# In the first layer, ScalarE makes the normalised input between the two exponentials of head six, and VectorE copies the fourth turn ahead of the low half of the source

## The reference, cut to what matters

```python
x = _gn(x)                                  # group norm, then in the layer:
x = _layernorm(x1d, norm_w, norm_b)         # per token
qkv = (x @ qkv_w.T).reshape(*x.shape[:-1], c, 3 * h)     # c = 32, h = 8 heads
q, k, v = (qkv[..., :h], qkv[..., h:2 * h], qkv[..., 2 * h:])
aff = jnp.einsum('bmich,bmjch->bmijh', q, k)
gate = jax.nn.sigmoid(x @ gate_w.T + gate_b).reshape(*x.shape[:-1], c, h)
bias = x2d @ x2d_w.T * factor
weights = jax.nn.softmax(aff + bias[:, None], axis=-2)
out = jnp.einsum('bmrch,bmirh->bmich', v, weights) * gate
out = out.reshape(*x.shape[:-1], c * h) @ final_w.T + final_b
```

## Time and profile before

| | |
|---|---|
| time, three runs | 3560.49 us median (3558.21 to 3562.08) |
| the profiled execution | 3560.76 us, span 3558.9 us |
| busy share of the span | PE 95%, PEld 84%, DVE 83%, ACT 77%, POOL 61% |
| mean granted TensorE clock | 0.971; 1.00 in both layers' steady stretches |
| DMA, mean over the span | 67 GB/s |

### The profile page before, as it was taken

How to read it: one execution, slowest core, us unless ns; L and a number is a source line. 1 busy time by engine, 2 the same in 40 slices (tenths; PEclk the granted TensorE clock), 3 DMA queues, 4 the chain that set the end, 5 groups by cost and what they waited for, 6 DMA issues and landing times.

```text
span 3558.9 us, 123057 instructions
## 1 busy us (share of the span) xinstructions
PE 3369.3 (95%) x36747; PEld 3001.8 (84%) x36747; DVE 2968.9 (83%) x10850; ACT 2753.6 (77%) x8999; POOL 2165.3 (61%) x4107
## 2 busy tenths in 40 slices
PE   4569999999999999999999999799999999999999
PEld 1148888888888888888888887799999999999998
DVE  4569999999999999999999998688888888888886
ACT  1149999999999999999999998567766667766666
POOL 0048888888888888888888886344444444443443
PEclk7579999999999999999999999899999999999999
DMA  9921111111111111111111111111111111111111
GB/s 356 370 91 54 53 48 49 53 50 48 53 53 44 53 53 46 51 53 53 44 53 53 44 53 34 42 51 53 53 53 53 50 50 53 53 53 53 51 49 49
DMA packets 189033, 238.42 MB, mean 67 GB/s; under 512 B 11825, under 2 KB 176177, under 8 KB 184753
## 3 DMA queue, kind: packets, MB, share of 16 engines
q1 hardware_dynamic: 184368, 204.17, 18.2%
q10 hardware_dynamic: 4608, 33.56, 2.5%
HBM read 170.57 MB, written 67.11 MB: 67 GB/s over the span
## 4 chain that ended last, share of the span: by engine, by line
PE 71%; DVE 9%; issue 8%; ACT 6%; DMA 4%; POOL 1%; DVEq 1%; SPq 0%; ACTq 0%; POOLq 0%
PE work L477 26%; PE work L486 11%; PE turn L538 7%; PE score L629 5%; PE score L508 5%; PE mix L662 4%; PE mix L550 4%; DMA x_chunk<-xT 4%; DVE prob L936 3%; ACT prob L734 3%; PE turn L646 3%; PE score L538 2%; ACT xnT L754 2%; PE turn L647 2%; PE turn L648 2%
## 5 line engine op out<-in xcount | busy, mean ns | idle before, releaser
L364 POOL TENSOR_SCALAR prob<-prob,row_inv 128x256 f32<-128x256 f32 x2048 | 1029.0, 522 | 213.0 <-DVE row_inv L942 211.5
L734 ACT ACTIVATE prob<-prob,row_min 128x256 f32<-128x256 f32 x2048 | 1022.0, 508 | 68.0 <-DVE row_min L936 61.4
L477 PE MATMUL work<-src,w 128*128 128x256 f32 x7680 | 1062.7, 287 | 10.3 <-DVE src L925 6.7
L477 PEld LDWEIGHTS work<-src,w 128*128 128x128 f32 x7680 | 946.9, 189 | 12.1 <-DVE src L925 7.4
L415 POOL TENSOR_SCALAR prob<-prob,row_inv 128x160 f32<-128x160 f32 x1024 | 391.1, 401 | 767.8 <-DVE row_inv L1055 767.8
L936 DVE CUSTOM_DVE_ANT_0 prob<-score,neg_bias 128x256 f32<-128x256 f32 x2048 | 756.9, 417 | 48.9 <-PE score L508 46.6
L799 ACT ACTIVATE prob<-prob,row_min 128x160 f32<-128x160 f32 x1024 | 431.2, 426 | 142.7 <-DVE row_min L1048 142.6
L538 PE MATMUL turn<-ident,prob 128*128 128x128 f32 x3072 | 471.9, 276 | 11.4 <-DVE probT L947 2.6
L486 PE MATMUL work<-w,src 128*128 128x256 f32 x3072 | 427.9, 288 | 9.7 <-ACT xnT L754 7.4
L477 PE MATMUL work<-att,wf 128*128 128x256 f32 x3072 | 432.6, 290 | 4.0 <-DVE att L1006 2.6
L538 PEld LDWEIGHTS turn<-ident,prob 128*128 128x128 f32 x3072 | 342.9, 141 | 85.0 <-POOL prob L364 45.3
(11 more groups left out here) (112 smaller groups left out, 6118.5 us busy)
## 6 DMA issues: line engine op xcount, KB each, us to landing
pair_chunk<-pairT ACTq DMA_DIRECT2D x32, 1024.0 KB, 7.7
x_chunk<-xT SPq DMA_DIRECT2D x32, 1024.0 KB, 8.4
x_tok<-x_nat SPq DMA_DIRECT2D x128, 256.0 KB, 3.3
x_sb<-xT SPq DMA_DIRECT2D x128, 256.0 KB, 3.4
x1T<-y_sb SPq DMA_DIRECT2D x128, 256.0 KB, 2.2
x_sb<-x1T SPq DMA_DIRECT2D x128, 256.0 KB, 2.9
outT<-y_sb SPq DMA_DIRECT2D x128, 256.0 KB, 2.2
prob<-w_d SPq DMA_DIRECT2D x1, 1024.0 KB, 8.2
```

What stands on the lines that cost most here:

```text
L364: pool.tensor_scalar(prob[:, h, ib], prob[:, h, ib], row_inv[:, h, ib:ib + 1], 1.0, ALU.mult, ALU.mult).then_inc(norm_done[0], 1)
L477: ins = pe.matmul(out[:, cb], w[:, of_w, kb, cols + cb * P:cols + (cb + 1) * P], x[:, of_x, kb], start=n == 0, stop=n == len(terms) - 1)
L734: act.activation(prob[:, h, ib], prob[:, h, ib], ACT.Exp, bias=row_min[:, h, ib:ib + 1], scale=-1.0, accum_out=row_sum[:, h, ib:ib + 1]).t ...
```

## The change

Two things are reordered, and nothing is added or removed. On ScalarE `exps(m, 5)` is split: its first half stays, `xnT` follows, and the second half comes after `xnT`, ahead of the key's high half. On VectorE the copy of turn 3 comes ahead of `split_low(0, far, ...)`. (Head six in the title counts from one: it is head 5 of the code.)

```diff
-                def exps(r, h):
-                    for ib in range(TB):
+                def exps(r, h, blocks=range(TB)):
+                    for ib in blocks:
...
-                    exps(m, 5)
+                    exps(m, 5, (0,))
                 if far.exists:
                     wait(act, t2_done, far.times(1, 1))
                     wait(act, src_done[0], far.times(1, 0))
...
                                        ).then_inc(xnT_done, 1)
+                if m.exists:
+                    exps(m, 5, (1,))
                 if nxt.exists:
                     wait(act, k_ps[0], nxt.times(1, 1))
...
+                if m.exists:
+                    turn_copy(3, turn[:])
                 if far.exists:
                     split_low(0, far, xnT[:])
-                if m.exists:
-                    turn_copy(3, turn[:])
                 if nxt.exists:
                     mins(nxt, 0)
```

## The result

The changed kernel takes 3679.8 us (median of 4 runs, 3679.03 to 3682.43) against 3559.35 us for the kernel before on the same chip: a ratio of 1.0338, 95% interval 1.0325 to 1.035. That is +120 us; forecast was +128 us, 3689 us. The profiled execution has a span of 3677.9 us.

The account below looks back on a forecast made before the run. TensorE was taken as nearly the bound, with turn 6 set by the row's first minimum. Collisions on VectorE and GpSimd make a pair of rows 33.26 us against 31.19: +2.07 times 62 pairs, +128 us, 3689 us; range 3575 to 3710.

Parts of the forecast that it names:

- What bounds the kernel: TensorE nearly the bound, busy 61.42 of 62.37 us; VectorE's slack before the row's first minimum leads to turn 6.
- The ScalarE edit: xnT 0.49 us earlier on ScalarE removes the value projection's wait: 0.28 us a row, 35 us at most.
- The displaced exponential: Head 5's second exponential starts 0.90 us after xnT; in rows 1 and 3 inverse at s (turn 6) + 9.90.
- TensorE's clock: From turn 6 (s): turn 2 at s + 9.41 or 9.38, turn 3 1.85 later; source's low half ready s + 12.57 or 12.54.
- GpSimd's clock: L380 starts at s + 12.08 and 12.38, 0.49 and 0.16 us before the source's low half is ready.
- rival 1: One of two effects missing: L925 wins in rows 2 and 4, 3633 us, or head 6's norm first, 3627; chance 0.20.
- The price of a collision: Source's low half waits out L380: next minimum at L380 + 1.76 us; price up to 1.07 us, the upper taken.
- The attention's low half: L1006 starts 1.53 us after the minimum and delays head 6: 2.64 us to turn 6 instead of 2.14.
- The sum: Rows of 16.48 and 16.78 us, a pair 33.26 against 31.19: +2.07, times 62 pairs, +128 us.
- Rival 3: No collision with L380 and none with L1006: a pair 30.77, 3535 us, lower bound 3526; chance 0.14.
- Rival 2: Source's low half not held up, L1006 still delays head 6: a pair 31.77, +36 us, 3597 us; chance 0.09.

Follow-up runs that it names:

- psum: Three timing-only kernels, att_psum, split_psum and both_psum: the changed kernel with one input of a low half, or of both, from PSUM; 3628.1, 3556.6 and 3510.8 us.
- best_neither: Kernel before with only two moves: GpSimd's sum L380 ahead of the norms, one layer-norm sum ahead of the attention's low half on VectorE; 3538.6 us.
- att_psum: Changed kernel, but the attention's low half reads the products in PSUM instead of their gated sum in SBUF (outputs not the layer's); 3628.1 us.
- pool_early: Changed kernel with GpSimd's sum L380 moved ahead of the norms of heads 4 and 5; 3559.4 us, ratio 1.0004.
- both_psum: Changed kernel with both low halves, the source's and the attention's, reading one input from PSUM (outputs not the layer's); 3510.8 us, ratio 0.986.
- split_psum: Changed kernel, but the source's low half reads products in PSUM in place of xnT (outputs not the layer's); 3556.6 us, ratio 0.9991.
- split_late: Changed kernel with the source's low half moved back on VectorE, behind the copy of turn 5; 3557.7 us, ratio 0.9996.
- best_old_scalar: Changed kernel, ScalarE edit undone, with GpSimd's L380 ahead of the norms and one layer-norm sum ahead of the attention's low half; 3555.5 us.

## Why the prediction was right

Time and cause came out as forecast: 120 us for 128, and the `psum` kernels show the collisions. By its own steps:

- **What bounds the kernel.** Right: what decided was the stretch from the minimum to turn 6. Keeping instructions of VectorE and GpSimd out of each other's way there is worth 22 us by itself, as `best_neither` shows.
- **The ScalarE edit.** Right in mechanism: the wait for `xnT` was covered. "35 us at most, if nothing later takes it back" was the right bound, and something takes it back: alone it gains 18 us, since turn 4 then waits 0.28 us for turn 3's copy. I had not seen that the attention's low half waits for ScalarE then and stays out of the way of head 6's norm.
- **The displaced exponential.** I gave it no price of its own, but the clock of L380 in rows 1 and 3 goes through it. Where the low half stands ahead of the copy, no price shows. On top of the VectorE edit, the ScalarE edit costs 31 us (3679.8 - 3648.5): with the exponential displaced, L380 starts at s + 12.11 instead of s + 11.56, and that puts it across the low half in the second kind of row too.
- **TensorE's clock.** Turn 2 starts at s + 9.38 (1037.95 - 1028.57; predicted 9.38) and turn 3 1.85 us later. The copy follows its end by 0.04 us (1040.44 - 1040.40), where I allowed 0.11, taken from ScalarE's copy. L927 starts at s + 12.47, predicted 12.54.
- **GpSimd's clock.** Inverse s + 10.20 (10.20), norms 0.38 later (0.37), L380 s + 12.39 (12.38). In the other kind of row L380 is at s + 12.11 (12.08). So it leads by 0.08 and 0.41 us where I had 0.16 and 0.49; the order, on which the forecast stood, is right. That the smaller lead had the right sign was in part luck: the working was off by 0.08 us, half of that lead, and the other way round it is rival 1 with 3633 us. The grouped row below (columns: mean ns of one after the comma) has every L380 at its undisturbed 1.28 us, so it comes first throughout:

```profile
L927 DVE TENSOR_TENSOR src<-xnT,src 128x512 fp32r<-128x512 f32 x111 | 175.5, 1581 | 0.0
L380 POOL TENSOR_TENSOR g_tok<-g_tok,gn_row 128x512 f32<-128x512 f32 x111 | 142.3, 1282 | 0.0
```

- **The price of a collision.** Predicted L380 + 1.76 to the minimum; 1.75 and 1.76 measured. The Trainium skill, "SBUF — State Buffer", section "SBUF: two separate sides", has the first to start hold the lock for its whole instruction; the trace agrees, and by that rule the instruction with one input in PSUM should be free of it, which it is (0.68 for 1.80 us).
- **The attention's low half.** Predicted 1.53 us behind the minimum and 2.64 us from there to turn 6; measured 1.44 and 2.60 (1045.31 - 42.71). That this low half holds up head 6 here is shown by `att_psum`, with 2.12. Rival 1's second half (head 6's norm first) did not happen in the changed kernel, but it did in `pool_early` in one row of four.
- **The sum.** Rows of 16.42 to 16.46 and 16.74 to 16.79 us against 16.48 and 16.78 predicted. A pair takes 33.19 (66.38 / 2) instead of 33.26, +2.00 for +2.07. 120 / 2.00 is 60 pairs where I had 62.

Two sizes in the rivals were off. Rival 3, the order with no collision, was put at 3535 us with 3526 as its floor; `both_psum` took 3510.8. Its step from the low half to the minimum was the low half's duration, 0.69 us, where the next instruction starts 0.60 us behind it (1008.01 - 1007.41 in `both_psum`), and its copy came 0.07 us too late, as said above. So its minimum stood at s + 13.23 to 13.26, and it came at s + 13.08 on average, with rows of 15.20 us instead of 15.37 and 15.40: about 22 us in 124 rows (0.18 a row). The floor of 3526 counted only the wait for `xnT`; the kernel before also waits for head 6's norm, 12.7 us in 29 rows. Rival 2, the attention's collision alone, was put at 3597 us; `split_psum` took 3557. The same two steps are in it, and in one row of four its race goes the other way, which costs VectorE 0.26 us and spares TensorE about half a us, some 15 us in all. In the forecast neither step shows, since there L380 sets the minimum. The separate prices are no sum either: 123 and 52 us alone, 169 together.

Not settled: how much of the miss on `split_late` (18 us) is the scores' new wait for the minima (21.4 us in its list) and how much is turn 6's wait for its norm (12.5 us). No run takes either away alone.

## What to carry to other kernels

Before an instruction is moved, look what runs on the other engines in its new slot: here a VectorE operation with both inputs in SBUF that became ready behind the start of a long GpSimd operation waited until that one had ended, and the trace shows it as a longer instruction, not as a wait. An engine's idle time ahead of a wait is only free while it stands where it is; work moved out of it onto the far side of the wait can come onto the path, as in `best_old_scalar`. When a collision is suspected, give one operand another home (PSUM) and leave the order alone: that tests the cause in one run, and a long operation of the other engine moved behind its short ones may cure it.

## What the runs showed of the hardware that was not expected

- How little a lead decides: GpSimd's instruction held up VectorE's with leads of 0.08 us (1040.96 and 1041.04) and 0.04 us (1054.38 and 1054.42, `att_psum`). VectorE's low half then ends about 1.83 us behind GpSimd's start whatever its own start was: 1040.96 + 1.83, 1024.22 + 1.83, 1028.29 + 1.83. So the earlier it is ready, the longer it is recorded.
- Short instructions in a row do not add up: among norms of about half a us each the same low half takes 0.69 to 0.77 us in `pool_early` (0.89 at 1770.69 in the kernel before), and behind one of 1.28 us it takes 1.4 to 1.8. GpSimd pays as well: where a low half falls among them, four norms take 2.28 to 2.31 instead of 1.85 us.
- The ends of the race need not be even: when L925 was 0.12 us ahead, L380 took 1.72 instead of 1.28 us, a loss of 0.44; the other way round VectorE loses up to 1.11 (1.80 in `att_psum` for 0.69).
